# Attention stack of a decoder kernel: the head norm's matmul behind the values on TensorE, and its logarithm behind the copy of the output on ScalarE

## The reference

```python
for i in range(DEPTH):                                       # 6
    x = attn_layer(shift_tokens(x), Wqkv[i], q_scale[i], k_scale[i], Wo[i]) + x
    x = ffn_layer(shift_tokens(x), ln_g[i], ln_b[i], W1[i], b1[i], W2[i], b2[i]) + x

def attn_layer(x, Wqkv, qs, ksc, Wo):
    q, k, v = jnp.split(x @ Wqkv, 3, -1)                     # 16 heads of 64
    q = l2norm(q) * qs
    k = l2norm(k) * ksc
    q = q * cos * scale + rotate_half(q) * sin * scale
    k = k * cos * inv + rotate_half(k) * sin * inv
    out = local_attention(q, k, v)                           # windows of 32, each sees itself and the one before
    return out @ Wo

def ffn_layer(x, g, bln, W1, b1, W2, b2):
    xn = (x - mu) / jnp.sqrt(var + 1e-05) * g + bln
    a, gate = jnp.split(xn @ W1 + b1, 2, -1)
    return a * jax.nn.gelu(gate, approximate=False) @ W2 + b2
```

## Time and profile before

| what | value |
|---|---|
| median of 3 runs | 1386.33 us (1385.07 to 1387.14) |
| the profiled execution's own time | 1383.36 us |
| its span, first to last instruction | 1381.5 us |
| mean granted TensorE clock | 0.945 of full speed |
| busy: PE, DVE, ACT, POOL | 85%, 68%, 61%, 48% |

### The profile page before, as it was taken

How to read it: one execution, slowest core, us unless ns; L and a number is a source line. 1 busy time by engine, 2 the same in 40 slices (tenths; PEclk the granted TensorE clock), 3 DMA queues, 4 the chain that set the end, 5 groups by cost and what they waited for, 6 DMA issues and landing times. The chain is left out here.

```text
span 1381.5 us, 27040 instructions
## 1 busy us (share of the span) xinstructions
PE 1176.7 (85%) x9636; PEld 730.0 (53%) x9636; DVE 945.4 (68%) x1207; ACT 838.4 (61%) x1260; POOL 660.0 (48%) x522
## 2 busy tenths in 40 slices
PE   7787789997648989898979988799887989999975
PEld 2222257775225655555555555556554555656551
DVE  2798857774746776776776676677766677777733
ACT  5554366664355667666766667576764667776744
POOL 1555434442246555545464554546454454645420
PEclk9899979999879999999999999999999999999997
DMA  3000043101113533434343433434333342434220
GB/s 104 1 0 0 1 123 122 56 6 47 45 31 84 144 82 93 106 98 107 75 108 76 127 80 85 105 98 106 77 86 97 99 106 75 106 96 107 70 61 15
DMA packets 75529, 107.32 MB, mean 78 GB/s; under 512 B 25348, under 2 KB 31939, under 8 KB 75003
## 3 DMA queue, kind: packets, MB, share of 16 engines
q1 hardware_dynamic: 75386, 105.47, 29.2%
HBM read 30.89 MB, written 0.59 MB: 23 GB/s over the span
## 5 line engine op out<-in xcount | busy, mean ns | idle before, releaser
L1667 POOL TENSOR_TENSOR st_sq_sum<-h 128x512 f32<-128x512 f32 x96 | 127.2, 1325 | 253.6 <-ACT h L1420 253.6
L1604 DVE TENSOR_REDUCE st_mx<-banks 128x8 f32<-128x512 f32 x96 | 66.4, 692 | 219.6 <-PE banks L1305 219.3
L1420 ACT ACTIVATE h<-banks 128x1024 f32<-128x1024 f32 x96 | 98.4, 1025 | 177.1 <-PE banks L1270 176.9
L1671 POOL TENSOR_TENSOR mo_w<-mo_w,x 128x512 f32<-128x512 f32 x96 | 122.3, 1274 | 160.0 <-DVE mo_w L1540 160.0
L1278 PE MATMUL banks<-st_sq_sum,head_ones 128*128 128x512 f32 x192 | 107.9, 644 | 43.3 <-POOL st_sq_sum L1667 43.2
L1290 PEld LDWEIGHTS banks<-st_wv,stream 128*128 128x128 f32 x768 | 101.5, 193 | 47.6 <-issue 46.6
L1550 DVE SCALAR_TENSOR_TENSOR st_turned<-st_rn,mo_w 128x1024 f32<-128x1024 f32 x96 | 121.1, 1262 | 6.3 <-ACT st_rn L1431 3.4
L1539 DVE TENSOR_TENSOR x<-banks,st_scaled 128x1024 f32<-128x1024 f32 x96 | 117.0, 1218 | 12.4 <-ACT h L1420 11.0
L1672 POOL TENSOR_TENSOR mo_w<-mo_w,x 128x512 f32<-128x512 f32 x96 | 122.4, 1275 | 0.0
L1329 PEld LDWEIGHTS banks<-st_p_blocks,st_vs 128*64 128x64 f32 x1536 | 78.1, 138 | 74.0 <-issue 71.8
L1540 DVE TENSOR_TENSOR mo_w<-banks,st_scaled 128x1024 f32<-128x1024 f32 x96 | 116.4, 1212 | 0.0
(11 more groups left out here) (230 smaller groups left out, 2662.6 us busy)
## 6 DMA issues: line engine op xcount, KB each, us to landing
st_qT<-st_turned SPq DMA_DIRECT2D x192, 128.0 KB, 2.4
st_k_blocks<-st_turned SPq DMA_DIRECT2D x384, 64.0 KB, 2.0
st_vs<-st_vn SPq DMA_DIRECT2D x96, 192.0 KB, 2.5
st_w_raw<-in_w_qk SPq DMA_DIRECT2D x12, 512.0 KB, 4.7
st_vs<-st_vn SPq DMA_DIRECT2D x96, 48.0 KB, 2.1
mo_w_all<-gate_rows SPq DMA_DIRECT2D x1, 3072.0 KB, 12.6
st_wv<-in_w_v SPq DMA_DIRECT2D x12, 256.0 KB, 3.0
st_wo<-in_wo SPq DMA_DIRECT2D x12, 256.0 KB, 2.9
```

The costliest lines, as they stand in the source:

```text
L1667: nc.gpsimd.tensor_tensor(sq_sum[:], sq[:, 0, :], sq[:, 1, :], ALU.add).then_inc(sq_summed.sem, 1)
L1671: nc.gpsimd.tensor_tensor(cos_part[:, which, 0, :], cos_part[:, which, 0, :], sin_part[:, 1, :], ALU.subtract).then_inc(add_done.sem, 1)
```

## The change

Two steps of a turn change places. On PE `head_norm` of unit t+4 moves from just behind `project_v` to just behind `values`. On ACT `logarithm` and `root` of unit t+4 move from before `copy_out` of unit t to just behind it. What each step computes and what it waits for stays as it is.

```diff
@@ -1393,8 +1393,6 @@
                     out_proj(s, t - 1)
                 if t >= -1 and s.unit(t + 1):
                     project_v(s, t + 1, job, stage)
-                if s.unit(t + 4):
-                    head_norm(s, t + 4)
                 if stage == 0:
                     mean(s, job)
                 if stage in (1, 2):
@@ -1403,6 +1401,8 @@
                     down(s, job)
                 if s.unit(t) and t >= 0:
                     values(s, t)
+                if s.unit(t + 4):
+                    head_norm(s, t + 4)
                 if stage == 1:
                     up_gate(s, t, job, 1)
 
@@ -1485,11 +1485,11 @@
                     copy_probs(s, t)
                 if t >= -1 and s.unit(t + 1):
                     copy_v(s, t + 1)
+                if t >= 0 and s.unit(t):
+                    copy_out(s, t)
                 if s.unit(t + 4):
                     logarithm(s, t + 4)
                     root(s, t + 4)
-                if t >= 0 and s.unit(t):
-                    copy_out(s, t)
                 if stage == 0:
```

## The result

| | kernel before | changed kernel |
|---|---|---|
| median, same chip | 1386.07 us (1385.07 to 1387.14, 4 runs) | 1404.22 us (1403.11 to 1405.98, 4 runs) |
| profiled execution, span | 1383.36, 1381.5 us | 1403.26, 1401.3 us |
| mean granted clock | 0.945 | 0.936 |

The ratio is 1.0135, 95% interval 1.012 to 1.015: slower, by 18 us. The forecast was 1404 us.

A forecast was written before the change was run, and what follows sets the result against it. In the attention stack the other engines mostly wait for PE. Terms 2.7 - 3.6 + 9.7 + 9.0 = +17.8 us on 1386.33 gave 1404 us, with a range of 1391 to 1412 and chance 0.62.

The forecast's parts named there:

- The sign and its reason: Plain turns: values wait for copies ending 0.26 us after the norm's sum; 0.85 for the kernel slower by over 0.2%.
- The rival in which the fill works: Copies ready when project_v ends, so values run during PE's wait for the sum: 1365 us, chance 0.09.
- the one in which one of the two large waits is hidden by another: After first or fourth feed-forward stage, VectorE or a transfer is late too; one 9 to 10 term goes: 1394, chance 0.12.
- the signs of being right: PE idle before L1278 under 10 us; dsq directly behind root; st_y_high late, first project waiting about 3 us instead of 2.
- The plain odd unit: Turns without feed-forward stage, odd t: the mask starts 0.16 us later in 17 units, +2.7 us.
- The late-sum units: First three units 0.7 us shorter each, five units t = 15 0.3 each, as values fit the norm's wait: -3.6.
- Stages 1 to 3: Second to fourth feed-forward stage: 0.27 us from second and third, counted within 0.9 for each of 10 jobs, +9.0.
- Stage 0: First feed-forward stage: dsq starts 0.88 us later, behind logarithm and root, 11 times, +9.7 us.
- The slow clock: Longer fourth-stage waits lower the granted clock in eight more of 21 units, 1.0 us each: 1412 us, chance 0.11.

The follow-up runs named there:

- e4_stage_turns: Kernel before with both moves made only in turns with a feed-forward stage, plain turns keeping the old order: 1414.67 us, ratio 1.018.
- e12_cast_early_after: Changed kernel with VectorE's cast of the next layer's weights put ahead of the heads' normalisation: 1408.9 us, ratio 1.015 to the kernel before.
- e9_best_mix: Mixed order against kernel before: changed order in plain turns, old in stages 1, 2; in 0, 3 norm behind values, logarithm and root last: 1366.72 us, 0.9874.

## Why the prediction was right, and where only its sum was

**The sign and its reason: shown.** The values have no less to wait for than the norm had. The wait moved from L1278 to L1329: 43.3 fell to 10.0, and 2.6 rose to 33.1 us. The rival in which the fill works did not happen, since the copies end behind the sum. Nor did the one in which one of the two large waits is hidden by another: `dsq` has no wait for VectorE left and `st_y_high` comes late, as the signs of being right had it.

**The plain odd unit: right for t = 5 and 7, too small for t = 13.** +0.25 instead of +0.16. The values start 0.14 after the copies and not 0.06, and the norm holds the mask for 0.97 and not 0.95. At t = 13 of the first five layers it was +0.85, since the copies ended 0.6 later behind `project_v` than the forecast took as fixed.

**The late-sum units: right for two, not for the rest.** The second and third unit gained 0.6 and 0.5 us, forecast 0.7. The first gained 2.1, but its turn was below the full clock before and is not now, and 1.3 came back at t = 5, so the first eight turns got 1.5 us shorter. The five units t = 15 gained nothing: the turns t = 0 that hold their norm are 2.1 us longer in sum, forecast -1.5. Why is open.

**Stages 1 to 3: right in sum, not in its parts.** For the jobs of the kind of t = 16, at full clock, the turn behind stage 1 got 0.48 longer, behind stage 2 0.12, behind stage 3 0.36: 0.96 a job against a forecast of 0.9. But 0.60 of it arose behind stages 1 and 2, where the forecast had 0.27, and less in stage 3. The `project` that waits for `st_y_high` waits 2.98 us, "about 3". The next square behind stage 1 came 1.37 later, forecast 1.2, and was hidden as forecast.

**Stage 0: the term that failed.** The step was "It now starts at 652.56, 0.88 later", times 11. For six of the eleven jobs it held nearly: `dsq` 0.70 later in four of the kind of t = 16 and 0.86 later in the two of the last layer. For the five of the kind of t = 24 it was earlier, 0.36 in four and 0.24 in the first. The working took the mean's start "at 647.81 as before" as fixed, and it was not: the residual ahead of it stood behind a cast stretched to 1.37 us by GpSimd, and the change happened to part the two. Where nothing is cast, in the last layer, the forecast's 0.88 nearly appears: 5.26 against 4.40 after `project_v`. `e4_stage_turns`, which keeps the collision, has 0.78. So the delay was real, and something that I did not look at paid for most of it: 4 x 0.70 + 2 x 0.86 - 4 x 0.36 - 0.24 = +2.8 instead of +9.7.

**The slow clock: a rival that came true in part.** It had a chance of 0.11 and eight more turns at 1.0 us each. Of t = 9 and t = 12 together ten turns are below the full clock instead of five, at 1.6 us each: 8 us; elsewhere two turns fewer are, and over the stack it is three more. For t = 12 the wait ahead did get longer, as the rival said (2.03 to 2.98). For t = 9 it did not (2.35, now 2.05), and why more of these turns are slow is open.

**The sum.** By turns of the two profiled executions, in us:

| turns | measured | forecast |
|---|---|---|
| the first eight | -1.5 | -2.1 |
| t = 5 to 8 | +4.3 | +2.7, with t = 13 |
| t = 1 and 9 (stage 0) | +6.1 | +9.7 |
| t = 2, 10 and t = 3, 11 (stages 1, 2) | +5.7 | +3.0 (0.27 a job) |
| t = 4 and 12 (stage 3) | +7.2 | +6.0, the rest of 9.0 |
| t = 13 to 15 | -7.3 | 0 |
| t = 0 (with the norm of t = 15) | +2.1 | -1.5 |
| all | +16.6 | +17.8 |

The spans differ by 19.8 us: 2.1 more arise ahead of these turns, in a part in which nothing was changed and the profiled executions of the experiments differ by -2.4 to +6.7 us, and 1.2 behind them.

So the total was met, and three entries behind it were not as argued. **Stage 0 is +6.1 only with two more slow turns in it (t = 9 has three more, t = 1 one fewer); without them it is 2.9, near the 2.8 above. t = 4 and 12 have two more as well; without them they are near 4. And t = 13 to 15 gave back 7.3.** One slow turn fewer is part of that; most is PE's wait for the transfer that places the keys, which in the turns t = 13 falls from 7.6 us in sum to 2.0. The long casts do not account for it: `e4_stage_turns` keeps them and is 6.5 shorter there, `e12_cast_early_after` has none and is only 1.6 shorter. What sets this wait was not tested. The delays in the stages and the sign are shown; that the missed stage 0 term and the gain at t = 13 to 15 nearly cancel with slow turns is luck.

## What to carry to other kernels

When two steps change places on an engine with a fixed order, compare when the inputs of both are ready, to a tenth of a microsecond: a wait does not go away when what takes its place is fed by the same source. Then look at who stands behind the moved step on the second engine; here the loss came in the stages, where `dsq` and `st_y_high` stand behind logarithm and root. In the mixed order, 1.3% faster than the kernel before, the largest single gain is in the turns that wait for `st_y_high`, which there goes ahead of the patient pair; for `dsq` the same step only avoided a loss. And before a start is called "as before", look whether the engines ahead of it touch each other: here a change of order elsewhere removed a collision of 1.1 us.

## What the runs showed of the hardware that was not expected

- **A VectorE cast can stand still for as long as a GpSimd operation lasts.** fp32 to fp32r, 128x256: 0.29 us alone, 1.37 when it started 0.05 behind GpSimd's sum, 1.35 when 0.32 behind (the sum itself then took 1.52), 0.54 behind a shorter subtraction; each ended 0.15 after the GpSimd row. Where the cast started first (by 0.19), neither was longer. The Trainium skill ("SBUF — State Buffer", section on who interferes with whom) says that a VectorE copy or cast in one of its two-port modes and a GpSimd instruction want the same pair of ports, and that the one issued second blocks until the first is done. The trace agrees for the cast that comes second. For the sum that comes second it shows little: with the cast 0.19 ahead the sum took its usual 1.27, with the cast 0.09 ahead 1.33.
- **The lower clock does not simply follow the length of the wait.** Of the six turns t = 9 none was below the full clock in `e9_best_mix`, where PE waits 1.30 us for `dsq` at t = 24, five in the changed kernel (2.05), but only two in the kernel before, where the wait is longest (2.35). Turns with the same instructions took 12.05 us at 1.00 and 13.65 at 0.87. What decides between them stays open.
- **Table loads on ACT** took 1.28 us, and the next activation began directly behind (672.70 + 1.28 = 673.98, and 674.00).
